# Vector products of a recommender tower read their layer input from SBUF instead of PSUM

## What is computed

```python
e = stack([tbl_f[ids[:, f]] for f in range(32)], axis=1)          # 1024 x 32 x 16
xk = x0 = e
for W in (W0, W1, W2):                                            # to 64 features each
    xk = relu(einsum('bmd,bhd,mhk->bkd', x0, xk, W))
    outs.append(sum(xk, axis=2))
h = concatenate(outs + [dense_ctx], axis=1)                       # 1024 x 208
h = maximum(h @ W_top1 + b_top1, 0)                               # 512
h = maximum(h @ W_top2 + b_top2, 0)                               # 256
y = h @ W_top3
```

## Time and profile before

| | |
|---|---|
| median of 3 runs | 628.99 us (628.71 to 633.98) |
| the profiled execution | 630.75 us |
| its span in the profile | 629.0 us |
| TensorE busy (matmul) | 606.1 us, 96% |
| VectorE busy | 514.3 us, 82% |
| GpSimd busy | 444.0 us, 71% |
| ScalarE busy | 322.1 us, 51% |

### The profile page before, as it was taken

One profiled execution on the slowest core, in us unless ns is written; L12 is line 12 of the kernel. 1 busy time (PEld: TensorE's weight loads), 2 busy tenths in 40 slices (PEclk: granted clock), 3 DMA queues, 4 the chain that ended last, 5 costly groups with the idle time before them and its releaser, 6 DMA issues.

```text
span 629.0 us, 8379 instructions
## 1 busy us (share of the span) xinstructions
PE 606.1 (96%) x2884; PEld 210.1 (33%) x2884; DVE 514.3 (82%) x454; ACT 322.1 (51%) x539; POOL 444.0 (71%) x346
## 2 busy tenths in 40 slices
PE   2788999999999999999999999999999999999998
PEld 1522333333333333333333333333333333333354
DVE  0058499999989998999999998999899998888600
ACT  1225546564636465564556463646546455643554
POOL 6777577878787878788787878787887876456400
PEclk9998999999999999999999999999999999999999
DMA  4886877877776768777678777677776767750000
GB/s 128 288 286 219 285 253 259 284 254 281 268 264 215 281 235 266 262 247 259 235 280 282 277 245 256 221 278 266 254 258 248 263 246 279 268 160 35 1 0 1
DMA packets 45199, 144.49 MB, mean 230 GB/s; under 512 B 9619, under 2 KB 24085, under 8 KB 32870
## 3 DMA queue, kind: packets, MB, share of 16 engines
q1 hardware_dynamic: 36966, 141.85, 62.3%
q0 software_dynamic: 8192, 2.11, 3.1%
HBM read 139.21 MB, written 4.72 MB: 229 GB/s over the span
## 4 chain that ended last, share of the span: by engine, by line
PE 95%; ACT 2%; DMA 1%; SPq 1%; DVE 1%; issue 0%; DVEq 0%
PE acc L658 68%; PE acc L650 13%; PE x_ps L624 5%; PE x_ps L691 2%; PE sums_ps L691 2%; PE acc L636 2%; DMA w_sb<-in_w 1%; PE acc L710 1%; ACT x_ps L520 1%; DVE dve_ring L579 1%; PE sums_ps L698 1%; PE acc L638 0%; ACT pair_squares L501 0%; PE sums_ps L705 0%; PE sums_ps L624 0%
## 5 line engine op out<-in xcount | busy, mean ns | idle before, releaser
L579 DVE TENSOR_TENSOR dve_ring<-x_wide,x_ps 128x1024 f32<-128x1024 f32 x428 | 488.2, 1212 | 62.1 <-issue 39.5
L658 PE MATMUL acc<-dve_ring,w_sb 128*64 128x512 f32 x1712 | 492.2, 595 | 5.8 <-DVE dve_ring L579 5.8
L460 POOL DMA_INDIRECT gathered<-in_table,idx x256 | 243.9, 953 | 69.6 <-issue 63.6
L472 POOL TENSOR_TENSOR pool_ring<-x_wide,x_sb 128x1024 f32<-128x1024 f32 x84 | 199.1, 2379 | 81.4 <-ACT x_sb L529 48.3
L658 PEld LDWEIGHTS acc<-dve_ring,w_sb 128*64 128x64 f32 x1712 | 155.1, 137 | 294.7 <-issue 273.4
L650 PE MATMUL acc<-pool_ring,w_sb 128*64 128x512 f32 x336 | 139.5, 592 | 0.0
L636 PE MATMUL acc<-pair_squares,w_sb 128*64 128x512 f32 x256 | 115.7, 592 | 2.4 <-ACT pair_squares L501 2.4
L520 ACT ACTIVATE x_ps<-acc 64x512 f32<-64x512 f32 x128 | 73.0, 570 | 77.9 <-PE acc L658 64.4
L524 ACT ACTIVATE layer_out<-acc 64x512 f32<-64x512 f32 x96 | 56.5, 588 | 60.3 <-PE acc L658 35.8
L501 ACT ACTIVATE pair_squares<-x_ps 128x1024 f32<-128x1024 f32 x32 | 32.8, 1026 | 98.3 <-PE sums_ps L624 98.3
L529 ACT COPY x_sb<-layer_out 64x512 f32<-64x512 f32 x128 | 79.0, 617 | 3.6
(11 more groups left out here) (36 smaller groups left out, 131.3 us busy)
## 6 DMA issues: line engine op xcount, KB each, us to landing
x_wide<-x_rows SPq DMA_DIRECT2D x96, 1024.0 KB, 7.8
x_wide<-x_rows SPq DMA_DIRECT2D x32, 768.0 KB, 5.6
x_wide<-x_rows SPq DMA_DIRECT2D x32, 256.0 KB
gathered<-in_table,idx POOLq DMA_INDIRECT x256, 5.4
x_rows<-gathered SPq DMA_DIRECT2D x32, 128.0 KB, 2.3
w_sb<-in_w SPq DMA_DIRECT2D x2, 512.0 KB, 5.1
x_rows<-gathered SPq DMA_DIRECT2D x32, 16.0 KB, 2.6
x_wide<-in_W_top SPq DMA_DIRECT2D x1, 512.0 KB, 6.4
```

Of the source, the lines that this page charges most:

```text
L460: pool.indirect_dma_start(gathered[:, c, j % 2, e * DIM:(e + 1) * DIM], None, table, bass.IndirectOffsetOnAxis(ap=idx[:, unit, e:e + 1], a ...
L472: nc.gpsimd.tensor_tensor(pool_ring[:, c], x0_step(c, j, layer, 2 * d, 2).rearrange("p (s n) -> p s n", n=COLS), x_sb[:, layer - 1, c, :]. ...
L579: nc.vector.tensor_tensor(dve_ring[:, c, slot:slot + width, :], x0_step(c, j, layer, i, width).rearrange("p (s n) -> p s n", n=COLS), x_ps ...
L658: done = nc.tensor.matmul(a, w, dve_ring[:, c, n % DVE_RING + i - at, :], start=first, stop=last)
```

## The change

VectorE's products read `x_sb` as GpSimd's do. `finish` writes its two relus straight into `x_sb` rather than into `x_ps`; the two copies from `layer_out` go. Since `x_sb` is now written earlier, `finish` waits for the products of the same thread's previous unit. `x_ps` goes; its place take two banks `more_sums_ps`, which with `sums_ps` are the four banks of `sums` for both threads (two of the eight banks are then unused), and the waits that shared banks needed go. The dense tower uses the four banks of the sums.

```diff
         sums_ps = psum("sums_ps", [P, 2, COLS])
-        x_ps = psum("x_ps", [P, 4, COLS])
-        BANK = {(2, 0): 0, (1, 1): 1, (2, 1): 2, (1, 0): 3}
+        more_sums_ps = psum("more_sums_ps", [P, 2, COLS])
...
-        mlp_banks = [sums_ps[:, 0, :], sums_ps[:, 1, :], x_ps[:, BANK[1, 0], :], x_ps[:, BANK[2, 0], :]]
+        mlp_banks = [ps[:, i, :] for ps in (sums_ps, more_sums_ps) for i in range(2)]
...
             def finish(layer, c, j):
                 a, h, tile = acc[j % 2], j % 2, j // 2
                 wait_layer(act, layer, c, j)
-
-                if layer == 0 and c == 0 and j > 0:
-                    act.wait_ge(squares_made, 3 * sum_number(1, j) + 1)
-                if layer == 0 and c == 1 and 0 < j < UNITS - 1:
-                    act.wait_ge(squares_made, 3 * sum_number(0, j + 1) + 1)
-                if layer == 1 and j < UNITS - 1 and (c, j) != (0, 0):
-                    act.wait_ge(squares_made, 3 * sum_number(c, j + 1) + 1)
                 if layer < 2:
+                    if j > 0:
+                        dve_last, pool_last = dve_before(c, j - 1, layer + 1, STEPS), pool_before(c, j - 1, layer + 1, STEPS)
+                        act.wait_ge(dve_made[c], dve_last)
+                        if pool_last:
+                            act.wait_ge(pool_made[c], pool_last)
                     for half in range(2):
-                        nc.scalar.activation(x_ps[out_half(half), BANK[layer + 1, c], :], a[out_half(c), :],
-                                             ACT.Relu).then_inc(x_ps_made[layer + 1][c], 1)
+                        nc.scalar.activation(x_sb[out_half(half), layer, c, :], a[out_half(c), :],
+                                             ACT.Relu).then_inc(x_sb_made[layer + 1][c], 1)
...
-                if layer < 2:
-                    act.wait_ge(out_made[layer][c], j + 1)
-                    for half in range(2):
-                        nc.scalar.copy(x_sb[out_half(half), layer, c, :],
-                                       layer_out[out_half(c), layer, h, :]).then_inc(x_sb_made[layer + 1][c], 1)
...
             def product(c, j, layer, i, width):
                 if i == dve_groups(c, j, layer)[0][0]:
-                    dve.wait_ge(x_ps_made[layer][c], 2 * (j + 1))
+                    dve.wait_ge(x_sb_made[layer][c], 2 * (j + 1))
...
                     x0_step(c, j, layer, i, width).rearrange("p (s n) -> p s n", n=COLS),
-                    x_ps[:, BANK[layer, c], :].unsqueeze(1).broadcast_to([P, width, COLS]),
+                    x_sb[:, layer - 1, c, :].unsqueeze(1).broadcast_to([P, width, COLS]),
...
             def sums(c, j):
...
-                if c == 0 and j > 1:
-                    pe.wait_ge(dve_made[0], dve_before(0, j - 1, 1))
-                    pe.wait_ge(dve_made[1], dve_before(1, j - 2, 2))
-                if c == 1 and j > 0 or (c, j) == (0, 1):
-                    pe.wait_ge(dve_made[0], dve_before(0, j - 1, 2))
-                    if j > 1:
-                        pe.wait_ge(dve_made[1], dve_before(1, j - 1, 1))
-                bank = sum_banks(c, j)
                 for q in range(SUM_TILES):
-                    to = x_ps[:, bank + q, :] if q < 2 else sums_ps[:, q - 2, :]
+                    to = (more_sums_ps if q < 2 else sums_ps)[:, q % 2, :]
```

More of the change, by code:

```diff
@@ L319, in cin_tower @@
         layer0_done = sems("layer0_done")
-        x_ps_made = {l: sems(f"x_ps_made{l}_") for l in (1, 2)}
         x_sb_made = {l: sems(f"x_sb_made{l}_") for l in (1, 2)}
@@ L362, in sum_number @@
             return THREADS * j + c
[L364 to L368, removed]
         def out_half(c):
@@ L499, in squares @@
                 act.wait_ge(sums_made, 4 * (n + 1))
-                bank = sum_banks(c, j)
-                nc.scalar.activation(pair_squares[:, c, 0:2, :], x_ps[:, bank:bank + 2, :],
-                                     ACT.Square).then_inc(squares_made, 1)
+                nc.scalar.activation(pair_squares[:, c, 0:2, :], more_sums_ps[:], ACT.Square).then_inc(squares_made, 1)
                 nc.scalar.activation(pair_squares[:, c, 2:4, :], sums_ps[:], ACT.Square).then_inc(squares_made, 1)
```

## The result

The changed kernel takes 803.2 us (median of 4 runs, 802.62 to 807.95) against 629.08 for the kernel before (4 runs); the ratio is 1.275, 95% interval 1.270 to 1.280. The span of the profiled execution is 801.8 us. The forecast was 786 us, slower.

The account below looks back on a forecast made before the run. It took TensorE to bound the kernel before and VectorE after the change: 50.07 us of start, 503.31 of VectorE's work, 196.69 of GpSimd's products, 34.53 of end and 1.75 for the profiled execution gave 786 us; range 709 to 880.

Parts of the forecast that it names:

- TensorE's reserve and VectorE's: In a pair of rounds before the change, TensorE was busy 68.40 of 68.40 us, VectorE 64.72, with 3.68 to spare.
- ScalarE's copies: On ScalarE, 128 copies into x_sb, 79.0 us, go; said to be worth nothing by itself.
- TensorE's waits: In `sums`, TensorE's waits for VectorE's reads of x_ps go; said to cost nothing before, so 0.
- the new waits in `finish`: Before overwriting x_sb, `finish` waits for the previous unit's products; said to be met when reached, 0.
- The product alone: A VectorE product with both inputs in SBUF, apart from any clash, was said to cost the same: 0.
- Full exclusion: VectorE stands for every microsecond of GpSimd's products in its window, 196.69 us; total 786 us, chance 0.50.
- GpSimd itself fits: In a pair of rounds of 88 us, GpSimd was said to need 76, including 12 for ten waits.
- the last rival: Gathers clash too: 220 gathers' 209.7 us come on top, 996 us in all; chance 0.05.
- hidden reductions: GpSimd products may run under VectorE's one-input reductions: 12 us, nearly cancelling about 11 us of VectorE idle time.
- VectorE first: VectorE keeps the path while it has work; GpSimd's product waits for a reduction or full ring: 859 us, chance 0.17.
- TensorE's clock: A fall in TensorE's clock could upset the forecast, but 45% of the time at 1.2 GHz was needed.

Follow-up runs that it names:

- layer-1 run: The changed kernel, but layer 1's input is also written to PSUM and VectorE reads it there, layer 2's still from SBUF: 736.6 us.
- few gathers: The changed kernel with seven of the eight gathers of each unit left out from unit 2 of a thread on: 777.1 us.
- two products: The changed kernel with two GpSimd products a round in place of five, VectorE making the other three: 726.3 us.
- single-step run: The changed kernel with VectorE's products of one step (512 elements) in place of two, 856 of them: 855.7 us.

## Why the prediction was right, point by point

- **TensorE's reserve and VectorE's.** Right: with TensorE full before, nothing could be gained, and VectorE's 3.68 us per pair of rounds were used up at once.
- **ScalarE's copies, TensorE's waits, the new waits in `finish`: 0 each.** Right. ScalarE's busy time fell by 78.6 us (322.1 to 243.5; 79 forecast) without effect, and ScalarE's waits after are for TensorE.
- **The product alone: 0.** Right: 583.8 us of busy time in SBUF against 583.4 in PSUM for the same 512 products. The cost of 62 cycles less that the Trainium skill (VectorE: DVE Perf Modes, The TRN2 errata) would give does not show.
- **Full exclusion.** Right in kind: 3.42 us for a VectorE product, 3.33 for a GpSimd one, only where both have two SBUF inputs, as the layer-1 run shows. This is the rule of the Trainium skill, SBUF — State Buffer, section Who interferes with whom (whoever starts first has the path for its whole instruction), and the trace agrees with it for each such pair in the changed kernel. Other runs don't always: VectorE products that started after a waiting GpSimd product ran ahead of it (few gathers, two products, single steps), and ten VectorE products of the layer-1 run and 38 of the single-step run stood for a GpSimd product that started 0.3 to 0.5 us after them. The term was too high: VectorE's products are busy 628.91 us in the window against 479.03, so they stand 150 us and not 196.69. 74 GpSimd products made VectorE stand, by 2.0 us each; eight of the other ten ran beside no VectorE product at all, and two beside the end of one.
- **"GpSimd itself fits".** Wrong, and the step that failed. The forecast let ten products wait and kept gathers at 0.95 us, "unless the last rival holds". The last rival asked only whether a gather holds VectorE up. It does not; but VectorE holds the gather up, by up to 1.03 us each. Per pair of rounds 32 gathers take 55.2 us and not 30.5, so GpSimd, with its gaps between gathers, needs 90 us and not 76. The one row used as evidence, a gather under a VectorE product of two SBUF inputs, overlapped only the gather's last 0.20 us, and the wait lies in its first 0.13.
- **Why the total came out all the same.** By luck: the two errors have opposite signs. The window was forecast at 700.0 us, all of it VectorE's own time and stands, with idle time and hidden reductions cancelling. It was 717.3: 653.1 busy, 47 less than forecast, and 64.2 idle, most of it because GpSimd's queue was late (26 without most of the gathers). The right total does not show the right bound: the run with few gathers does, where VectorE is the bound and the time is 777.1.
- **VectorE first** had 0.17 and did not come true here, but its mechanism is real, as the single-step run shows. What decides at the end of a VectorE product whether GpSimd's waiting product gets in was not settled: it does in the changed kernel each time, and does not at least 14 times in the single-step run, eight times in the run with few gathers and for the product of 19.33 us in the run with two products.
- **TensorE's clock** was named as a risk. The granted clock in a pair of rounds fell from 1.00 to 0.94 (some of it at 1.2 in place of 2.4 GHz), behind waits of up to 4.9 us for GpSimd's product. TensorE was busy 77.63 of 90.34 us there, 86% and not the 77% of the forecast, and has 12.7 us left over. Whether it added to the time by slowing the steps that give a ring place back to GpSimd was not tested.

## What to carry to other kernels

Where VectorE and GpSimd work at the same time, look at where each two-input operation of VectorE has its operands: one operand in PSUM kept the two apart here, and a copy that looks redundant may be there for that. Price such a clash for both engines and for everything in both queues, gathers issued by GpSimd among them, and not only for the pair of instructions that one thinks of. If VectorE must read both operands from SBUF, try the kernel without GpSimd's arithmetic: here it was 116 us faster.

## What the runs showed that was not expected

A gather on GpSimd's queue takes 0.94 us alone and up to 1.98 beside VectorE products with two SBUF inputs, and the wait follows the length of the VectorE product (0.52 us at most with products of 0.68 us). It doesn't hold VectorE in turn: 512 VectorE products beside such gathers had a busy time within 0.4 us of those beside gathers of 0.94 us. Only where a GpSimd product came right behind the gather, in the ten places of the layer-1 run and the 38 of the single-step run, did a VectorE product that started under a gather stand, and then for the product too. The Trainium skill, SBUF — State Buffer, section Who interferes with whom, infers that a `tensor_tensor` on VectorE does not stall descriptor generation on GpSimd, since it takes only the read interface of the shared path. It says nothing of a gather, whose indices lie in SBUF (`idx`); here the gather stood, so for it the measurement decides.

Smaller VectorE products made the sharing worse, not better: GpSimd's products waited up to 17.33 - 2.37 = 15 us, through 25 VectorE products, until VectorE did something that reads one operand or had to wait itself. The size of the products isn't the whole of it: with products of full length and few for GpSimd one waited 17 us.
